# Two half-width additions on GpSimd in place of one, in an attention kernel

## The reference

```python
def _L0_attn_ref(queries, Wq, Wkv, Wout, bout):
    ...
    q, k = (_rope(q), _rope(k))
    sim = jnp.einsum('bhid,bhjd->bhij', q, k) * SCALE
    attn = jax.nn.softmax(sim, axis=-1)
    out = jnp.einsum('bhij,bhjd->bhid', attn, v)
    out = out.transpose(0, 2, 1, 3).reshape(b, n, HEADS * DIM_HEAD)
    return out @ Wout + bout
...
x = x + _L0_attn_ref(_layernorm(x, axis=-1), ...)
x = x + _L0_ffn_ref(_layernorm(x, axis=-1), ...)
```

## Time and profile before

| | before |
|---|---|
| median of three runs | 1434.36 us |
| the profiled execution | 1434.8 us |
| its span, first to last instruction | 1433.0 us |
| PE busy | 1376.5 us, 96% of the span |
| VectorE busy | 1171.0 us, 82% |
| GpSimd busy | 975.7 us, 68% |
| ScalarE busy | 788.7 us, 55% |

### The profile page before, as it was taken

The page is one execution under the profiler, slowest core; times in us unless marked ns, Lnnn a source line. Parts: engine busy times, 40 slices in busy tenths (PEclk is TensorE's granted clock), DMA queues, the critical chain, the costliest instruction groups (busy, mean ns, idle before and its releaser), DMA issues.

```text
span 1433.0 us, 25611 instructions
## 1 busy us (share of the span) xinstructions
PE 1376.5 (96%) x7313; PEld 501.8 (35%) x7313; DVE 1171.0 (82%) x1318; ACT 788.7 (55%) x1511; POOL 975.7 (68%) x489
## 2 busy tenths in 40 slices
PE   3789999999999999999999999999999999999897
PEld 1223233333324333332433333342333334233334
DVE  6878888888788888878888888888888887889944
ACT  3345555555565555555555555555555555555555
POOL 4596866768486677858677685858668684865741
PEclk9799999999999999999999999999999999999999
DMA  6304131221403122230312222031312204131001
GB/s 186 64 1 87 33 83 22 59 59 31 86 17 81 24 58 58 47 72 15 81 37 62 41 59 59 15 81 37 78 25 59 59 19 86 29 81 23 16 16 59
DMA packets 72258, 75.47 MB, mean 53 GB/s; under 512 B 36036, under 2 KB 37576, under 8 KB 72104
## 3 DMA queue, kind: packets, MB, share of 16 engines
q1 hardware_dynamic: 71944, 74.56, 23.3%
q10 hardware_dynamic: 288, 0.59, 0.1%
HBM read 22.04 MB, written 2.35 MB: 17 GB/s over the span
## 4 chain that ended last, share of the span: by engine, by line
PE 49%; issue 22%; POOL 18%; DVE 7%; ACT 2%; DMA 1%; POOLq 1%; ACTq 0%; DVEq 0%
PE O L398 17%; PE S L386 9%; PE S L387 8%; POOL SA L696 7%; POOL T L666 5%; PE M L409 5%; PE TILE L316 3%; PE TILE L340 3%; DVE MX L616 3%; POOL YR L669 3%; POOL STAGE L683 3%; ACT PF L523 1%; PE TILE L332 1%; PE TILE L322 1%; DVE ST L267 1%
## 5 line engine op out<-in xcount | busy, mean ns | idle before, releaser
L696 POOL TENSOR_TENSOR SA<-PF 128x1024 f32<-128x1024 f32 x254 | 656.4, 2591 | 363.6 <-DVE SUM L623 304.8
L523 ACT ACTIVATE PF<-S 128x512 f32<-128x512 f32 x1024 | 556.1, 597 | 439.0 <-PE S L387 437.4
L616 DVE TENSOR_REDUCE MX<-M 128x1 f32<-128x1024 f32 x510 | 599.8, 1217 | 160.2 <-PE M L409 159.3
L398 PE MATMUL O<-PF,V 128*64 128x512 f32 x2048 | 496.5, 606 | 0.0
L386 PE MATMUL S<-QK 128*128 128x512 f16 x1024 | 393.4, 384 | 9.1 <-ACT PF L523 9.1
L387 PE MATMUL S<-QK 128*128 128x512 f16 x1024 | 389.6, 380 | 0.0
L626 DVE TENSOR_TENSOR SUM<-SUM,SA 128x1024 f32<-128x1024 f32 x126 | 229.6, 1822 | 7.1 <-POOL SA L696 6.0
L398 PEld LDWEIGHTS O<-PF,V 128*64 128x64 f32 x2048 | 124.4, 136 | 249.6 <-issue 173.4
L386 PEld LDWEIGHTS S<-QK 128*128 128x128 f16 x1024 | 99.2, 97 | 262.6 <-ACT PF L523 113.3
L409 PE MATMUL M<-QK 64*128 64x512 f16 x1020 | 161.8, 394 | 5.8 <-DVE MX L616 5.2
L505 ACT ACTIVATE OS<-O 64x512 f32<-64x512 f32 x128 | 75.7, 591 | 83.3 <-PE O L398 82.6
(11 more groups left out here) (118 smaller groups left out, 745.2 us busy)
## 6 DMA issues: line engine op xcount, KB each, us to landing
QK<-STAGE SPq DMA_DIRECT2D x128, 256.0 KB, 3.9
QK<-STAGE SPq DMA_DIRECT2D x128, 128.0 KB, 3.1
RB<-den SPq DMA_DIRECT2D x124, 128.0 KB, 3.0
X<-in_L_attn_queries SPq DMA_DIRECT2D x4, 512.0 KB, 10.7
QK<-MN SPq DMA_DIRECT2D x128, 1.0 KB, 2.0
out<-X SPq DMA_DIRECT2D x8, 256.0 KB, 2.0
RT<-DS SPq DMA_DIRECT2D x124, 2.0 KB, 1.7
WRAW<-in_L_attn_Wkv SPq DMA_DIRECT2D x2, 512.0 KB, 8.0
```

The lines of the kernel that those rows point to most:

```text
L398: mm = e.matmul(O[DH * z:DH * z + DH, :], V[:, h, kt * DH:(kt + 1) * DH], PF[:, t % SLOTS, z * HALF:(z + 1) * HALF], start=(kt == 0), stop ...
L523: e.activation(PF[:, t % SLOTS, z * HALF:(z + 1) * HALF], S[:, z * HALF:(z + 1) * HALF], ACT.Exp, scale=EXP_SCALE).then_inc(exped, 1)
L616: e.tensor_reduce(MX[:, place % 2, q:q + 1], bank, AX, ALU.max).then_inc(max_read, 1)
L696: e.tensor_tensor(SA[:, (t // 2) % 2, :], PF[:, t % SLOTS, :], PF[:, t % SLOTS + 1, :], ALU.add).then_inc(two_summed, 1)
```

## The change

In place of one addition of 1024 columns, which waits until all four halves of the two tiles are there, POOL runs two additions of 512 columns. Each waits for the exponentials of its own half (`exped` at 3 or 4 above four times the pair). The wait for the buffer of SA now stands ahead of both. Only the second adds to `two_summed`, so VectorE is told of a pair when both halves are done. The arithmetic is the same.

```diff
         def pool_sum(e, t, pair, free):
 
-            e.wait_ge(exped, 4 * pair + 4)
             wait(e, summed, free)
-            e.tensor_tensor(SA[:, (t // 2) % 2, :], PF[:, t % SLOTS, :], PF[:, t % SLOTS + 1, :],
-                            ALU.add).then_inc(two_summed, 1)
+            for z in range(2):
+                half = slice(z * HALF, (z + 1) * HALF)
+                e.wait_ge(exped, 4 * pair + 3 + z)
+                both = e.tensor_tensor(SA[:, (t // 2) % 2, half], PF[:, t % SLOTS, half], PF[:, t % SLOTS + 1, half],
+                                       ALU.add)
+            both.then_inc(two_summed, 1)
```

## The result

The changed kernel took 1439.61 us (median of six runs, 1438.87 to 1440.46) against 1434.33 for the kernel before (six runs): a ratio of 1.0038, interval 1.0028 to 1.0048, or +5.3 us. It is slower by more than the 0.2% that can be told from no change. The forecast was +3.8 us.

The account below looks back on a forecast made before the run. PE bounds the kernel, busy 82.45 of 82.60 us a loop iteration. Loop +3.3, first iteration +1.1, last -0.6 make +3.8 us: 1438.2 against the median of 1434.36, range 1434.2 to 1442.0 (own range +2.4 to +5.2).

Parts of the forecast that it names:

- The bound and the place: Loop: PE is the bound, standing 0.32 us once an iteration behind ACT's copy of YR; any delay there is paid 14 times.
- A sum grows by 0.15 us: Each POOL sum: two halves take 2.46 us instead of 2.31, +0.15, between 0 and +0.35.
- The moved wait costs 0.07: Start of a POOL sum: waiting for `summed` one queue instruction earlier adds 0.07 us, between 0 and 0.14.
- L626 absorbs 0.1, and YR is 0.24 late: Loop: L626 waits about 0.1 us for STAGE, the second sum adds 0.15, YR ends 0.24 late; 14 x 0.24 = +3.3 us.
- The first iteration costs 1.1: First iteration: six sums in POOL's chain give 0.9, VE and following waits 0.2; together +1.1 us, between 0.6 and 1.5.
- The last iteration gains 0.6: Last iteration: VE enters between the halves 0.9 us earlier, two sums hold VectorE up 0.3; together -0.6 us, down to -1.3.
- VectorE's shorter waits are worth nothing in the loop: Loop's other 14 sums: VectorE waits less for POOL, at most 1.26 us instead of 2.36, but PE never waits for VectorE.
- The sum: Whole kernel: loop, first and last iteration together +3.8 us, 0.27% more; this forecast had chance 0.72.
- halves were not free: Rival at each sum: second half nearly free, +0.02 us a sum, 1434.4 us, no change; chance 0.10.
- no gap opened between them: Rival at each sum: a gap between the halves, +0.35 us a sum, 1445.3 us, with half the gap 1441.9; chance 0.10.
- the second rival: Loop: POOL's first half precedes the ready L626, which runs at the seam; YR ends 0.6 us earlier, 1429.7 us; chance 0.08.

Follow-up runs that it names:

- The quarters: Four additions of 256 columns a sum in place of the changed kernel's two halves: 1453.88 us, ratio 1.0143 against the kernel before.

## Why the prediction was right, and where it was not

- *The bound and the place.* Right. PE stands once an iteration behind the third YR, without cover; splitting two sums alone reproduces the loop's cost, splitting the fourteen others does not, and moving the third copy, and with it the fourth that then takes its place, removes it.
- *A sum grows by 0.15 us.* 0.14 measured; 1269 ns a half at the median. The quarters confirm the price for each instruction. The Trainium skill's figures (GPSIMD Engine Reference, "Elementwise"), by which I had estimated 0.06, gave too little.
- *The moved wait costs 0.07.* 0.10 in the trace. Alone it costs next to nothing, since L626 takes it up; beside the split, which needs the same 0.1 us, it is paid.
- *L626 absorbs 0.1, and YR is 0.24 late.* It waited 0.14, YR was 0.29 late. The step is right; the moved wait was sized 0.03 short and L626's wait 0.04, and 14 times the missing 0.05 is most of the difference between the forecast's loop (14 x 0.24, which is 3.4 and not the 3.3 of the sum) and +4.12.
- *The first iteration costs 1.1.* Not settled: the run with only this part split gives +0.9 with an interval that takes in zero, and +0.9 between profiles with the same granted clock, one of them split. The terms of its sum were not taken apart.
- *The last iteration gains 0.6.* Wrong, the one step that failed: "VE can go in at the seam, [...] some 0.9 us earlier". It did, by 1.0, but I had followed only that instruction. L289 behind it met the second half and gave 1.0 back (1.10 before, 2.13 now). What stayed is a loss: +0.95 in the changed kernel, of which +0.7 is the last iteration's own. Part of it is VectorE's additions waiting for longer sums, for which the forecast had 0.3: with only the last iteration split, one L626 (at 1378.04) waits 0.45 us for its sum and takes 2.27, where it took 1.46 without a wait (at 1377.05), and PE waits 0.19 us behind the L550 after it, where it had no wait. The rest is not traced.
- *VectorE's shorter waits are worth nothing in the loop.* Right: the loop with the fourteen others split is not shorter (+0.20).
- *The sum.* +3.8 was forecast, +5.3 measured, 0.1 above the end of the forecast's own range (+2.4 to +5.2). The steps that carry it are the predicted ones; by the marks the loop gave 0.8 more than forecast and the last iteration 1.6 more, with the other sign. The parts, 4.1, 0.9 and 0.95, add up to 0.7 more than the medians differ, inside the interval of that difference (4.0 to 6.9 us).

The rivals fell on rows: halves were not free, no gap opened between them (2.49 us for two of about 1.26), and POOL did not go ahead of a waiting L626. But the idea in the second rival, that a changed order of YR and VectorE's addition is worth more than any instruction's price, came true at another place and with the opposite sign: 0.4 us an iteration lost when, with split sums and the third copy later, the fourth YR fell behind SUM.

## What to carry to other kernels

Before splitting an instruction so that its first part may start earlier, look at what ended the waits in front of it: if it is never the data that arrives in halves, the split has only its price, here 0.14 us for each instruction more on GpSimd and 0.10 for the wait that it moved. Ask for that price where the bound engine waits, not over the whole program; 2 of 16 places carried it all. And where a wait is shortened at a seam, follow the instruction behind it on the same engine, which meets the rest. The cheaper fix was to look from the waiting side: one copy moved behind the work that the bound engine needs gave 5 us with whole sums, 0.9962 of the time before (0.9948 to 0.9975), the lowest median here.

## What was not expected of the hardware

VectorE's L289, a subtraction and multiplication of one 128 x 128 tile by two values a partition, was held up by GpSimd like the two-input additions: 2.13 us for four beside the second half, 1.10 without. The prediction had counted VE (L278), the addition of a constant to four values a partition, among what GpSimd holds up, but not L289 right behind it. That a `tensor_scalar` can take the ports shared with GpSimd is what the Trainium skill states (SBUF — State Buffer, "Who interferes with whom"), and the trace agrees.
